# A graph network whose edge planes are scattered by GpSimd: the order of the setup work, and which rounds of the scatter wait for which

## What is computed

```python
def _L0_gnn_ref(x, edge_row, edge_col, edge_vals, eps, W1, b1, g1, be1, W2, b2, g2, be2):
    msgs = edge_vals[:, None] * x[edge_col]
    agg = jax.ops.segment_sum(msgs, edge_row, num_segments=n)
    h = (1.0 + eps[0]) * x + agg
    h = _bn_relu(h @ W1 + b1, g1, be1)
    h = _bn_relu(h @ W2 + b2, g2, be2)
    return h
```

## Time and profile before

| | |
|---|---|
| median of 3 runs | 3699.06 us |
| lowest and highest run | 3691.95 and 3702.07 us |
| span of the profiled execution | 3699.5 us |
| granted TensorE clock, mean over the span | 0.962 |
| TensorE busy | 91% |
| VectorE busy | 62% |
| ScalarE busy | 23% |
| GpSimd busy | 22% |

### The profile page before, as it was taken

The page is one execution under the profiler, slowest core; times in us unless marked ns, Lnnn a source line. Parts: engine busy times, 40 slices in busy tenths (PEclk is TensorE's granted clock), DMA queues, the critical chain, the costliest instruction groups (busy, mean ns, idle before and its releaser), DMA issues. The chain is left out here.

```text
span 3699.5 us, 34277 instructions
## 1 busy us (share of the span) xinstructions
PE 3370.1 (91%) x12633; PEld 1924.8 (52%) x12633; DVE 2307.1 (62%) x3045; ACT 841.0 (23%) x1111; POOL 802.9 (22%) x652
## 2 busy tenths in 40 slices
PE   6999867687999999999929999999999999997998
PEld 6897646464555455455524444444444444464444
DVE  9972322236111102343698888888888899968987
ACT  0103322234100000133112222222222223242222
POOL 3788888870000000000011111111111100010000
PEclk9999988898999999999959999999999999998999
DMA  9999978896343444321455555555555432284422
GB/s 354 366 278 237 283 169 242 219 256 144 126 132 125 132 136 132 111 80 53 123 169 142 131 128 123 135 118 130 135 119 132 111 97 67 60 295 145 123 63 68
DMA packets 279137, 572.59 MB, mean 155 GB/s; under 512 B 93394, under 2 KB 157672, under 8 KB 276922
## 3 DMA queue, kind: packets, MB, share of 16 engines
q1 hardware_dynamic: 140777, 432.89, 36.8%
q0 software_dynamic: 85712, 77.51, 13.3%
q10 hardware_dynamic: 52480, 60.01, 6.0%
HBM read 365.44 MB, written 204.87 MB: 154 GB/s over the span
## 5 line engine op out<-in xcount | busy, mean ns | idle before, releaser
L1202 PE MATMUL ps<-R,B 125*128 125x500 f32 x2800 | 1092.9, 541 | 33.3 <-DVE R L2118 27.3
L1202 PEld LDWEIGHTS ps<-R,B 125*128 125x128 f32 x2800 | 503.3, 190 | 595.7 <-issue 551.6
L711 POOL DMA_INDIRECT pairs<-w x400 | 618.7, 1547 | 195.3 <-issue 142.7
L1041 PE MATMUL ps<-R,H 125*128 125x500 f32 (+1 forms) x1400 | 543.4, 543 | 15.1 <-ACT H L1299 7.6
L1426 ACT ACTIVATE R<-R,asc 125x1625 f32<-125x1625 f32 (+1 forms) x200 | 320.2, 1601 | 989.1 <-DVE R L2105 989.1
L2105 DVE SCALAR_TENSOR_TENSOR R<-H,asc 125x1625 f32<-125x1625 f32 (+1 forms) x200 | 368.9, 1846 | 143.9 <-PE ps L1209 113.4
L2118 DVE SCALAR_TENSOR_TENSOR R<-R 125x1625 f32<-125x1625 f32 (+1 forms) x250 | 444.9, 1779 | 0.0
L1041 PEld LDWEIGHTS ps<-R,H 125*128 125x128 f32 x1400 | 253.5, 191 | 284.0 <-issue 281.0
L894 PE MATMUL ps<-R,H 125*128 125x375 f32 (+1 forms) x1000 | 304.4, 452 | 95.5 <-DMA R<-pairs 95.1
L1672 DVE TENSOR_TENSOR Fb<-Fb,ps 128x250 f32<-128x250 f32 (+1 forms) x140 | 67.2, 480 | 360.7 <-PE ps L894 278.0
L741 POOL DMA_DIRECT2D den_d<-R x138 | 119.2, 863 | 794.5 <-DVE R L2118 766.1
(11 more groups left out here) (316 smaller groups left out, 3039.6 us busy)
## 6 DMA issues: line engine op xcount, KB each, us to landing
pairs<-R SPq DMA_DIRECT2D x25, 3200.0 KB
R<-ct_d SPq DMA_DIRECT2D x162, 406.2 KB, 3.5
R<-pairs SPq DMA_DIRECT2D x25, 2500.0 KB
R<-ct_d SPq DMA_DIRECT2D x162, 375.0 KB, 3.2
R<-wt_d SPq DMA_DIRECT2D x50, 812.5 KB, 4.4
R<-wt_d SPq DMA_DIRECT2D x50, 750.0 KB, 4.2
den_d<-R POOLq DMA_DIRECT2D x75, 312.5 KB, 5.6
den_d<-R POOLq DMA_DIRECT2D x75, 250.0 KB, 4.8
```

The source lines that it names most:

```text
L711: pool.indirect_dma_start(pairs, bass.IndirectOffsetOnAxis(ap=key_u[:, c:c + 1], axis=0), val[:, c, :], None, compute_op=ALU.add)\
L1041: last = mm(ps[:, bank, at:at + w], rows[0:Q, j, f * 128:(f + 1) * 128], TL[q % TS][0:Q, o:o + w], start=j == 0 and at == 0, stop=j == NB ...
L1202: last = mm(ps[:, bank, at:at + w], rows[0:Q, j, f * 128:(f + 1) * 128], TT[q % TR][0:Q, o:o + w], start=j == 0 and at == 0, stop=j == NB ...
```

## The change

- **SP**: the 16 KB tail and the first two zero blocks (`ZAHEAD = 2`) are issued ahead of features, small values and `w01`.
- **VectorE**: keys are made first, then block bounds, then `span`. The clears of the staging tiles go to ScalarE, the clear of `val`, the first fill of `key_u`, the counts in `vals` and the trash rows to GpSimd. ScalarE writes the first part of the weights, GpSimd the other two.
- **Step 0 of the merge** is done in halves: after six comparisons the first four columns are merged (semaphore `first_merged`), the others in step 1, now ahead of its second comparison. Round 0 waits only for the first half.
- **Range test** after step 0 in place of step 1. It also writes `rfirst`: for round k of 1 to 5 the value 2k + 1 if the ranges touch, else 1. ScalarE counts `early_ok` up by one whenever half a round has landed, in order; GpSimd adds 1 at the start. Round k waits for `early_ok` to reach its value.
- Feature statistics begin at step 6 (`STAT0`) in place of 3. TensorE multiplies step 0 ahead of the key rows of step 1.

The fixed waits `first_two(k-2)`, `last_two(k-2)` and `first_two(k-1)` stay, and so does `ZQ = 4`.

```diff
@@ SP
-            for p0, p1 in PART:
-                sp.dma_start(X[p0:p1, :, :], x.rearrange("(j p) f -> p j f", p=Q)[p0:p1]).then_inc(S("x_in"), 16)
...
+            def features_in():
...
             for i in range(NB + ZQ):
+                if i == ZAHEAD:
+                    features_in()
                 if i >= ZQ:
                     sp.wait_ge(S(f"zeroed{i % ZQ}"), 16 * (i // ZQ))
                     sp.sem_inc(S("zero_ok"), 1)
@@ GpSimd
+            pool.sem_inc(S("early_ok"), 1)
...
+            pool.wait_ge(S("wgt_split"), 2)
+            link(g.tensor_tensor(r1, wgt, vals[:, :, 0], ALU.subtract))
+            link(g.tensor_copy(vals[:, :, 1], r1))
+            link(g.tensor_tensor(r2, r1, vals[:, :, 1], ALU.subtract))
+            g.tensor_copy(vals[:, :, 2], r2).then_inc(S("vals_made"), 1)
...
             for k in range(NMG):
-                if k % 2 == 0:
+                if k == 0:
+                    pool.wait_ge(S("first_merged"), 1)
+                elif k == 1 or k % 2 == 0:
                     pool.wait_ge(S("merged"), k // 2 + 1)
...
-                if k == LAND + 2:
-                    pool.wait_ge(S("rwait_made"), 2)
-                if 1 <= k < LAND + 2:
-                    first_two(k - 1)
-                    last_two(k - 1)
+                if k == 1:
+                    pool.wait_ge(S("rwait_made"), 3)
+                if 1 <= k <= FIRST_ROUNDS:
+                    landed_first = pool.value_load(rfirst[0:1, k - 1:k], min_val=1, max_val=2 * FIRST_ROUNDS + 1)
+                    pool.wait_ge(S("early_ok"), landed_first)
+                    pool.sem_inc(S("begun"), 1)
@@ ScalarE
+            a(WSTF[0][96:128, :], nothing.to_broadcast([32, 4 * PW]), ACT.Copy).then_inc(S("stage_clear"), 1)
...
+            for r in range(FIRST_ROUNDS):
+                act.wait_ge(S(f"first_two{r % LAND}"), 32 * (r // LAND + 1))
+                act.sem_inc(S("early_ok"), 1)
+                act.wait_ge(S(f"last_two{r % LAND}"), 32 * (r // LAND + 1))
+                act.sem_inc(S("early_ok"), 1)
@@ VectorE
-            link.mark(v_.memset(val, 0.0))
-            link.mark(v_.memset(keyd, 0.0))
-            link.mark(v_.memset(small[:, 1:2], 0.5))
-            for t in WSTF + CSTF[1:]:
-                link.mark(v_.memset(t[96:128, :], 0.0))
-            v_.memset(PT[96:128, :], 0.0).then_inc(S("stage_clear"), 1)
...
+            link.mark(stt(erow, e2, 128.0 - Q, e1, ALU.mult, ALU.add))
+            dve.wait_ge(S("src_in"), 16)
+            link(cp(esrc, src_i))
+            stt(key_c, erow, float(ROW), esrc, ALU.mult, ALU.add).then_inc(S("edge_dve"), 1)
...
+                    if t == 0 and c == MG + 1:
+                        merged(0, 0, MG, "first_merged")
+                    if t == 1 and c == 0:
+                        merged(0, MG, SC)
...
+                    link(stt(low[:, 0:f_], near[:, 1:f_ + 1], 2.0, tnum[0:1, 0:f_], ALU.mult, ALU.mult))
+                    ts(rfirst[0:1, 0:f_], low[:, 0:f_], 1.0, None, ALU.add).then_inc(S("rwait_made"), 1)
```

More of the change, by code:

```diff
@@ L32 @@
 ZR = 10
+ZAHEAD = 2
+STAT0 = 6
 MG = 4
@@ L270, in gnn_stack @@
         keyf = sb("keyf", [128, 2, SC])
-        e1f, e2f = [Fb[0:Q, k * CW:k * CW + EC] for k in (4, 5)]
+        e1f, e2f = [Hf[0:Q, k * CW:k * CW + EC] for k in (2, 3)]
         bneed = sb("bneed", [128, NMG], I32)
@@ L443, in gnn_stack, with sum_bank @@
         LAND = 4
+        FIRST_ROUNDS = LAND + 1
         PART = [(0, 112), (112, Q)]
+        def sum_bank(t, c):
+            return 7 if t == 0 and c < MG else 4 + t % 2
         ZREG = 64
@@ L814, in _ @@
             tr = nc.tensor.transpose
[L815 to L822, removed]
             pe.wait_ge(S("wgt_in"), 16)
             for a in range(EA):
-                tr(ps[0:Q, 4, a * ECC:(a + 1) * ECC], key_c[:, a * Q:(a + 1) * Q], ident[0:ECC, 0:ECC])
+                last = tr(ps[0:Q, 5, a * ECC:(a + 1) * ECC], wgt_c[:, a * Q:(a + 1) * Q], ident[0:ECC, 0:ECC])
+            last.then_inc(S("edge_pe"), 1)
+            pe.wait_ge(S("edge_dve"), 1)
             for a in range(EA):
[L827 to L830, removed]
+                last = tr(ps[0:Q, 4, a * ECC:(a + 1) * ECC], key_c[:, a * Q:(a + 1) * Q], ident[0:ECC, 0:ECC])
+            last.then_inc(S("edge_pe"), 1)
+            pe.wait_ge(S("edge_dve"), 2)
+            tr(ps[0:1, 7, 0:ECC], bmax[0:ECC, 0:1], ident[0:ECC, 0:ECC])
+            tr(ps[0:1, 7, ECC:2 * ECC], bmin[0:ECC, 0:1], ident[0:ECC, 0:ECC]).then_inc(S("edge_pe"), 1)
+            pe.wait_ge(S("edge_dve"), 3)
             def key_rows(t):
@@ L848, in sums @@
                     for c in range(c0, c0 // MG * MG + MG):
-                        last = mm(ps[0:Q, 4 + t % 2, c * 4:(c + 1) * 4], TW[c0][:, c * Q:(c + 1) * Q],
-                                  vals[:, t * SC + c0, :], start=c0 == 0 and c == 0, stop=c0 == c, skip_group_check=True)
+                        last = mm(ps[0:Q, sum_bank(t, c), c * 4:(c + 1) * 4], TW[c0][:, c * Q:(c + 1) * Q],
+                                  vals[:, t * SC + c0, :], start=c0 == c and (c == 0 or t == 0 and c == MG), stop=c0 == c,
+                                  skip_group_check=True)
                     last.then_inc(S("same_used"), 1)
             key_rows(0)
+            pe.wait_ge(S("edge_dve"), 4)
+            for i in range(4):
+                last = tr(ps[0:1, 6, i * ECC:(i + 1) * ECC], span[0:ECC, i:i + 1], ident[0:ECC, 0:ECC])
+            last.then_inc(S("edge_pe"), 1)
+            pe.wait_ge(S("vals_made"), 1)
             for t in range(NSC):
-                if t + 1 < NSC:
-                    key_rows(t + 1)
+                if t:
+                    key_rows(t + 1) if t + 1 < NSC else None
                 sums(t)
+                if t == 0:
+                    key_rows(1)
             pe.wait_ge(S("merged"), NSC)
@@ L1284, in _ @@
             a = nc.scalar.activation
-            act.wait_ge(S("edgeT"), 1)
-            a(wgt.rearrange("p (c i) -> p i c", i=EA), ps[0:Q, 5, 0:EC].rearrange("p (i c) -> p i c", i=EA), ACT.Copy)\
-                .then_inc(S("edges_laid"), 1)
+            act.wait_ge(S("zero_made"), 1)
+            nothing = R[96:128, 0:1]
+            a(WSTF[0][96:128, :], nothing.to_broadcast([32, 4 * PW]), ACT.Copy).then_inc(S("stage_clear"), 1)
+            act.wait_ge(S("edge_pe"), 1)
+            wgt_rows = ps[0:Q, 5, 0:EC].rearrange("p (i c) -> p i c", i=EA)
+            a(vals[:, :, 0].rearrange("p (c i) -> p i c", i=EA), wgt_rows, ACT.Copy).then_inc(S("wgt_split"), 1)
+            a(wgt.rearrange("p (c i) -> p i c", i=EA), wgt_rows, ACT.Copy).then_inc(S("wgt_split"), 1)
+            for t in WSTF[1:] + CSTF[1:] + [PT[:, :]]:
+                a(t[96:128, :], nothing.to_broadcast([32, t.shape[1]]), ACT.Copy).then_inc(S("stage_clear"), 1)
+            for r in range(FIRST_ROUNDS):
[3 more added lines that the diff above has]
+                act.sem_inc(S("early_ok"), 1)
             def normalise(l, half, dst):
@@ L1302, in _ @@
             normalise(0, 0, H)
-            act.wait_ge(S("stage_clear"), 1)
+            act.wait_ge(S("stage_clear"), 4)
             act.wait_ge(S("rneed_made"), 1)
-            act.wait_ge(S("rwait_made"), 2)
+            act.wait_ge(S("rwait_made"), 3)
             for n, (what, g, x_) in enumerate(HW_SEQ):
@@ L1496, in _ @@
             v_.memset(R[:, 0:2 * ROW // ZR], 0.0).then_inc(S("zero_made"), 1)
-            link.mark(v_.memset(val, 0.0))
-            link.mark(v_.memset(keyd, 0.0))
-            link.mark(v_.memset(small[:, 1:2], 0.5))
-            for t in WSTF + CSTF[1:]:
-                link.mark(v_.memset(t[96:128, :], 0.0))
-            v_.memset(PT[96:128, :], 0.0).then_inc(S("stage_clear"), 1)
+            link.mark(v_.memset(later[:, :, :], 0.0))
             v_.memset(ones[:, :], 1.0).then_inc(S("ones_made"), 1)
@@ L1520, in _ @@
             link(v_.tensor_reduce(out=span[0:ECC, 3:4], in_=e1[:, Q:CW], axis=AX_X, op=ALU.min))
[L1521 to L1527, removed]
+            dve.sem_inc(S("edge_dve"), 1)
+            dve.wait_ge(S("trash_made"), 1)
+            dve.wait_ge(S("edge_dve"), 3)
+            both = trash[:, :, :].rearrange("p a i -> p (a i)")
+            link.mark(tt(keyd.rearrange("p (t i) -> p t i", i=2 * SC), key.rearrange("p (t i) -> p t i", i=2 * SC),
+                         both[0:Q, :].unsqueeze(1).to_broadcast([Q, NSC // 2, 2 * SC]), ALU.subtract))
+            dve.wait_ge(S("edge_pe"), 3)
             ts(bneed[0:1, :], ps[0:1, 7, 0:ECC], 1.0, None, ALU.add).then_inc(S("need_made"), 1)
+            dve.wait_ge(S("pool_consts"), 9)
             link.mark(cp(bminf[0:1, :], ps[0:1, 7, ECC:2 * ECC]))
[L1530 to L1550, removed]
             dve.wait_ge(S("ones_made"), 1)
+            dve.wait_ge(S("stage_clear"), 1)
             def same(t, c):
@@ L1563, in same, with merged @@
                     ALU.is_equal, ALU.mult, accum_out=later[0:Q, t % 2, c:c + 1]).then_inc(S("same_made"), 1)
-            def merged(t):
```

(22 more changed lines are left out.)

48 lines of the change are left out of this document (32 added, 16 removed).

## The result

| | before | changed |
|---|---|---|
| median, lowest, highest run | 3697.57 (3691.95 to 3702.07, 4 runs) | 3663.23 (3657.62 to 3668.34, 4 runs) |
| span of the profiled execution | 3699.5 | 3659.2 |

The changed kernel takes 0.9907 of the time of the kernel before (95% interval 0.9895 to 0.9919): 34.3 us less by the medians. 3663 us was forecast. The kernel before had a fourth run here, which moved its median from 3699.06 to 3697.57 us. The profiled execution took 3660.92 us, 1.7 us over its span.

What follows compares the result with a forecast made beforehand. GpSimd's scatter sequence, with layer 0 behind it, was taken as the limit. From 3699.5 us, -35.3 - 1.0 + 0.6 = -35.7 gave 3663.8; the runs' median lies 0.4 below the span, so 3663, range 3650 to 3676.

Steps and rivals of the forecast that it cites:

- The limit: From the third late group on, layer 0 follows GpSimd's scatter rounds; a microsecond gained there is one of the span.
- Range wait, -35.3 us: Rounds 1 to 5 on GpSimd: idle stretches of 36.8 us go, less the usual 5 x 0.3.
- Landings as the next stay, +0.6: Fixed landing waits in the early rounds, now dense, cost 0.6 us for 20 more issues; bounds 0 and 10 us.
- Rival 2: Landings become new stalls: dense early rounds wait at their fourth issue; 3673 us, chance 0.07.
- First scatter, -1.0 us: First issue at 37.5 us, held by SP's report of a zeroed block at 36.5; bounds +2 and -17.4 us.
- the dip of the DMA rate at 12 to 20 us: 214 GB/s where 410 are possible; if this 3.8 us dip goes, the zeroed-block report comes at 33 us.
- Rival 1: Zero gate opens early because SP's issues return sooner; fully 16.4 us less, 3647 us, chance 0.10.
- The merge near 19 us and without effect: First merge done near 19 us, without effect because the first scatter waits for the zeroed-block report.
- Rivals 3 and 4: 3: VectorE holds 21 issues, 15 us, 3679, chance 0.03. 4: change doesn't act, 3698 to 3700, chance 0.04.
- Rival 5: Shifted waits bring TensorE's lower clock into the matrix-bound part, 43 us lost: 3706 us, chance 0.03.
- The range of the own case: The prediction's main case, 3658 to 3670 us by its bounds, chance 0.73.

Runs made afterwards that it cites:

- e3: Changed kernel with ZQ = 2 and the first zeroed block reported ahead of the features: 3642.47 us over five executions, 0.9851 without the profiled one.
- e5: The kernel of e3 run once more for an undisturbed profile: 3643.33 us, 0.9856 of the kernel before.
- e1: Changed kernel, but rounds 1 to 5 again wait until all four scatters of the round before have landed: 3697.75 us, 1.0002 of the kernel before.
- e7: Kernel before with the range wait, ZQ = 2 and first report ahead of features, but old setup and whole first merge: 3664.72 us, 0.9911.
- e9: Kernel of e3, but GpSimd starts its clears and casts only when VectorE has finished the keys: 3645.27 us, one execution.
- e8: Kernel of e3, but round 0 waits for the whole first merge step in place of its first half: 3650.04 us, 0.987 of the kernel before.

## Why the prediction was right, point by point

- **The limit** (GpSimd's issues, then layer 0 behind them): held. The last scatter began at 780.9 in place of 816.4, 35.5 us earlier, and the medians differ by 34.3. Over all profiled kernels but e3 the last release of SP (the end of the line's range in the release lines below) moved from 770.2 (e5) to 827.2 us (before), and from there to the end it was always 2866 to 2874 us. That the hit is within 0.3 us is luck: the gain came 1.4 us smaller than the 35.7 of the sum, and the median that it is taken from 1.5 us lower.
- **Range wait, -35.3 us**: held. Start of round 0 to start of round 5 took 37.30 us in place of 72.55, so -35.25.
- **Landings as the next stay, +0.6**: it measured nothing, and so small a term is within noise. A scatter landed in 7.5 to 7.7 us in the early rounds, under the 11.1 that were worked out as free. They had one landing wait, of the usual 0.3 us, and from round 5 to the last scatter the changed kernel took 704.9 us and the kernel before 705.3. Rival 2 is refuted.
- **First scatter, -1.0 us**: the mechanism was right, the size slightly off. It came 0.16 us later, the report at 37.8 where 36.5 was taken. The step that was off is that the dip of the DMA rate at 12 to 20 us might go: it moved. The DMA engines carry 401 GB/s there now, and 264 at 20 to 30 us and 234 at 30 to 38.5. As an estimate from the bytes, 6.8 MB had moved by 20 us and edges and two blocks are 7.2 MB, so the dip is where the features go. Rival 1 is refuted for this change, and e5 shows its price, 20 us (16.4 was worked out, from a first scatter at 21 us; it came at 19.54).
- **The merge near 19 us and without effect**: 18.02. That its 18 us lay hidden behind the gate is shown by e1, e5 and e7 together.
- **Rivals 3 and 4**: refuted. The 21 early issues took 1545 ns in the median and at most 1816 (1797 before), and the waits went. That each issue would lose a VectorE operation (21 x 0.73 us) is a term that no run shows.
- **Rival 5**: didn't happen. From 264 us to the end the granted clock, as a share of the full one, was 0.96 in the mean in both kernels. The clock rows of the first 260 us need care, below.
- **The range of the own case**, 3658 to 3670: its terms don't give this. With the report at 33 and no landing term the sum is 3659.7, with the first scatter 2 us later than before 3666.8.
- **The profiled pair** differs by 40.3 us. Of this 35.5 are the last scatter and 2.7 the wait for its landing (10.8 and 8.1 us from its start to SP's release), from the release lines of before and after:

```profile
L490 SPq EVENT_SEMAPHORE  x8: 17/17/17, 259.9 to 827.2; - x8
```

```profile
L504 SPq EVENT_SEMAPHORE  x8: 17/17/17, 249.9 to 789.0; - x8
```

  The other 2 us lie behind and are less than the runs of one kernel differ by.

## What to carry to other kernels

Before rewriting the work ahead of a first issue, list everything that this issue waits for and when each came, not only the one that the profile names. Here two came 0.8 us apart, so an 18 us shorter setup was worth nothing until a small change to the other (when a queue reports what has long landed) let it through. A report that stands behind further issues in a full queue comes when those are through (37.8 us here), not when the thing reported is done (13.4).

## What the runs showed of the hardware

**An order of transfers on a full queue.** From 4 to 20 us the DMA share was 1.03 to 1.04 in the changed kernel. The second feature transfer took SP 14.15 us to issue with zero blocks ahead of it; the same transfer took 8.14 in the kernel before, with edges and the larger feature transfer ahead. The second zero block, with little ahead, took 1.41 us, and the 25 of this kernel 9.0 in the median. In e5, where SP waits for a block to land before it issues the next but one, the median is 0.51 us. So in these rows the issue is slow by what stands before it.

**VectorE beside GpSimd.** A 100x500 cast took 1.65 us beside GpSimd's cast into `key_u` and the clear behind it, 0.42 us without them (e9); in e5 it was the third step that took 1.19 us beside that clear, 0.42 in e9; the trash subtraction 1.06 us beside a GpSimd cast, 0.58 before and in e9. The prediction had set GpSimd's share at no cost to VectorE; it was hidden here only by the gate. The long step ended 0.29 us after GpSimd's clear of the counts both times (5.45 and 5.16 us in the changed kernel, 5.98 and 5.69 in e5). The scatters' issues stayed at 1545 ns in the median, with VectorE busy for 40.38 of 41 us (34 to 75 us of the changed kernel). GpSimd itself needed 1.05 to 1.08 us for each of the four steps on 125x400 values that took VectorE 0.57 to 0.61.

**The granted clock's rows of the first 250 us don't always fit the pace.** The row 34 to 75 us of the changed kernel says 0.50, of the kernel before say 1.00 up to 250 us. Here are the changed kernel's row, eight transposes of 125x125 in the kernel before at 101 us and eight at 803 us, in a stretch of 1.00, and eight of the changed kernel at 101 us:

```profile
34.00:75.00 41.00, 36.66 (x239) 35.60 (x239) 40.38 (x187) 0.00 (x0) 30.54 (x20) 0.50 1.11 365
```

```profile
101.03 2.02 PE L838 MATMUL ps<-ident,Fb 125*125 125x125 f32 x8
...
803.36 1.09 PE L914 MATMUL ps<-ident,R 125*125 125x125 f32 x8
```

```profile
100.66 2.02 PE L867 MATMUL ps<-ident,Fb 125*125 125x125 f32 x8
```

Both kernels transposed at the same pace there, about half of the later one (2.02 us for eight, 1.09 later), so the 1.00 of the kernel before doesn't fit its pace in that stretch, and the two means over the span (0.962 and 0.934) don't say that the changed kernel ran slower. Runs of one kernel fall into both groups with the same time: on e1's chip the kernel before took 3695.60 us with a mean of 0.932 and 3695.26 with 0.963. And e8's rows say 1.00 for 75 to 250 us where e9's say 0.50, with TensorE busy for 161.35 and 161.31 us. In e3's profiled execution they say 1.00 from start to end, with matmuls of more than twice the usual time (1274 ns, 542 in the changed kernel). In the scatters' stretch the slower pace cost these two kernels nothing, since a merge step had 14.8 us (eight scatters) and took about 4.6 (two merges of the changed kernel end at 122.4 and 127.0 us). In e5, where the first merge holds the first scatter, no run shows what it costs. Why the records differ was not tried.
